# Rotary operands projected once in a four-layer diffusion transformer, with pair swaps on VectorE, sine products on GpSimd, and one exponential instruction a bank

## The reference, cut to what matters

```python
def _rope(x, sin, cos):
    xe = x[..., ::2]
    xo = x[..., 1::2]
    re = xe * c - xo * s
    ro = xe * s + xo * c
    return jnp.stack((re, ro), axis=-1).reshape(x.shape)
...
q = _rope(q, sq, cq)
k = _rope(k, sk, ck)
sim = jnp.einsum('bhnd,bhmd->bhnm', q, k) * DH ** (-0.5)
a = jax.nn.softmax(sim, axis=-1)
o = jnp.einsum('bhnm,bhmd->bhnd', a, v)
```

## Time and profile before

| what | value |
| --- | --- |
| median of 3 runs | 5925.9 us (5922.57 to 5927.59) |
| the profiled execution | 5942.8 us |
| its span, first to last instruction | 5941.0 us |
| mean granted TensorE clock | 0.951 of full speed |
| instructions | 164056 |
| busy share: TensorE, VectorE, ScalarE, GpSimd | 91%, 74%, 55%, 43% |
| HBM traffic | 19 GB/s over the span |

### The profile page before, as it was taken

One profiled execution on the slowest core, in us unless ns is written; L12 is line 12 of the kernel. 1 busy time (PEld: TensorE's weight loads), 2 busy tenths in 40 slices (PEclk: granted clock), 3 DMA queues, 4 the chain that ended last, 5 costly groups with the idle time before them and its releaser, 6 DMA issues. The chain is left out here.

```text
span 5941.0 us, 164056 instructions
## 1 busy us (share of the span) xinstructions
PE 5433.4 (91%) x66584; PEld 3128.8 (53%) x66584; DVE 4393.0 (74%) x6682; ACT 3259.3 (55%) x5626; POOL 2543.8 (43%) x2193
## 2 busy tenths in 40 slices
PE   5899999999999999999999999999989999999967
PEld 4554555555455455555545546565544545556442
DVE  6887776667888867576888886767788887767633
ACT  3455566565455566656455555655555555665634
POOL 2643535444344444444344344444534445344420
PEclk8998999999899999999999999999999999999975
DMA  4010010101001000010100101010100100101000
GB/s 104 12 40 17 14 29 9 37 12 41 18 16 43 13 26 19 21 25 17 43 13 26 31 11 34 12 32 15 35 22 14 38 17 15 29 10 36 10 17 6
DMA packets 282335, 145.67 MB, mean 25 GB/s; under 512 B 151517, under 2 KB 266813, under 8 KB 281470
## 3 DMA queue, kind: packets, MB, share of 16 engines
q1 hardware_dynamic: 281598, 135.17, 9.4%
HBM read 112.39 MB, written 3.01 MB: 19 GB/s over the span
## 5 line engine op out<-in xcount | busy, mean ns | idle before, releaser
L2459 DVE TENSOR_REDUCE max_part<-ring 128x2 f32<-128x800 f32 (+2 forms) x2304 | 2264.7, 1011 | 647.4 <-PE ring L1599 640.8
L2097 ACT ACTIVATE probs<-ring 128x1024 f32<-128x1024 f32 (+1 forms) x2048 | 1949.1, 969 | 1326.0 <-PE ring L1599 837.9
L1575 POOL TENSOR_TENSOR weight_sum<-weight_sum,probs 128x512 f32<-128x512 f32 (+1 forms) x1408 | 1825.2, 1296 | 350.4 <-ACT probs L2097 217.9
L1575 POOL TENSOR_TENSOR weight_sum<-probs 128x512 f32<-128x512 f32 x256 | 330.2, 1290 | 1984.6 <-ACT probs L2097 1564.5
L1599 PE MATMUL o_acc<-probs,region 128*64 128x256 f32 (+1 forms) x6656 | 908.3, 393 | 6.1 <-ACT probs L2097 3.2
L1599 PE MATMUL ring<-qop,region 64*128 64x256 f16 x9984 | 779.8, 271 | 22.8 <-DVE max_part L2459 8.2
L1599 PEld LDWEIGHTS ring<-qop,region 64*128 64x128 f16 x9984 | 450.8, 95 | 244.3 <-issue 118.8
L1599 PEld LDWEIGHTS o_acc<-probs,region 128*64 128x64 f32 (+1 forms) x6656 | 415.9, 137 | 281.3 <-issue 140.1
L1599 PE MATMUL o_acc<-probs,x_nv 128*32 128x256 f32 x6656 | 501.7, 420 | 37.0 <-ACT probs L2097 34.0
L1599 PE MATMUL ring<-shift_q,shift_k 64*128 64x256 f16 (+1 forms) x3840 | 529.8, 270 | 0.0
L2483 DVE RECIPROCAL o_inv<-ring 128x256 f32<-128x256 f32 x256 | 447.2, 1750 | 87.8 <-PE ring L1599 87.4
(11 more groups left out here) (191 smaller groups left out, 6966.3 us busy)
## 6 DMA issues: line engine op xcount, KB each, us to landing
stage<-in_wide SPq DMA_DIRECT2D x448, 64.0 KB, 2.0
nk<-x_nk SPq DMA_DIRECT2D x768, 25.0 KB
wo_stage<-in_wide SPq DMA_DIRECT2D x32, 512.0 KB, 4.0
ff_w<-in_ff_w SPq DMA_DIRECT2D x48, 256.0 KB, 3.5
stage<-in_wide SPq DMA_DIRECT2D x64, 128.0 KB, 2.6
v_stage<-in_wide SPq DMA_DIRECT2D x128, 64.0 KB, 2.0
ff_w<-in_ff_w SPq DMA_DIRECT2D x16, 512.0 KB, 3.7
v_stage<-kv_split SPq DMA_DIRECT2D x128, 48.0 KB, 1.7
```

The lines of the kernel that those rows point to most:

```text
L1575: pool.tensor_tensor(total, before, probs[0:rows_, (un.chunk + k) % PROBS, :], ALU.add)\
L2097: act.activation(to, src, ACT.Exp, scale=t.scale).then_inc(exp_done.sem, 2)
L2459: dve.tensor_reduce(dst, src, AX.X, ALU.max).then_inc(*release(one))
```

## The change

The change has five parts.

1. Each rotary operand is projected once. The swapped weights are no longer loaded or split; a rotary unit stages two pieces of weights instead of three, and `kv_in` for sub 1 is loaded in two parts instead of three.
2. VectorE makes the partners out of the one bank: `stream_shuffle` copies it to the new tile `swapped`, with neighbouring partitions exchanged, and the cosine product follows out of the same bank. Both tiles have two slots.
3. GpSimd multiplies `swapped` by the sines and then adds it to `raw`. ScalarE's high copy waits for that addition.
4. The exponential is one instruction a bank, 512 elements, and each bank is free when its own is done. Scores no longer need neighbouring banks; maxima still do.
5. The planner's costs follow these parts, and all tables of due times are replaced.

The diff, cut to its core:

```diff
-            return [("op", o, r) for r in range(2 if self.rope else 1)]
+            return [("op", o, 0)]
...
 AFTER = {
-    0: {"load": 1.499, "stats": 4.424, "ln": 4.629, "ctx": 0.522},
+    0: {"load": 2.2618, "stats": 4.2102, "ln": 2.1272, "ctx": 4.0025},
...
 PACE = {
-    0: 8.043, 1: 28.0, 6: 6.711, 7: 24.852, 3: 6.44, 4: 21.0, 9: 6.0, 10: 21.008
+    0: 9.5689, 1: 28.1233, 6: 7.0255, 7: 25.9515, 3: 7.0734, 4: 21.0636, 9: 6.0, 10: 21.0393
...
             if t.rope:
-                if k == 0:
-                    at = ROPE_OPS.index((n, i))
-                    before = ROPE_OPS[at - 2] if at >= 2 else None
-                    deps = [("DVE", ("job", before[0], low_job(UNITS[before[0]].t, before[1])))] if before else []
-                    self.part("DVE", "rope", due, one, 0.03 + w * 0.00142, [pe, *deps])
-                    return
-                self.part("DVE", "rope", (due[0], due[1] - 0.5), ("sin", n, j), 0.03 + w * 0.00142, [pe])
-                self.part("DVE", "rope", due, one, 0.05 + w * 0.00142, [("DVE", ("sin", n, j)), ("DVE", ("job", n, j - 1))])
-            self.part("ACT", "op", due, one, 0.17 + w * 0.00083, [("DVE", one) if t.rope else pe])
...
+                self.part("DVE", "rope", first, ("swap", n, j), 0.09 + w * 0.00112, [pe, *swapped])
+                self.part("DVE", "rope", due, ("cos", n, j), 0.03 + w * 0.00142, [pe, *free])
+                self.part("POOL", "rope", first, ("sin", n, j), 0.08 + w * 0.0025, [("DVE", ("swap", n, j))])
+                self.part("POOL", "rope", due, one, 0.08 + w * 0.0025, [("POOL", ("sin", n, j)), ("DVE", ("cos", n, j))])
+            self.part("ACT", "op", due, one, 0.17 + w * 0.00083, [("POOL", one) if t.rope else pe])
...
-            if paired(what):
+            if is_max(what):
                 r = min(side_by_side(), key=lambda r: beside(r) + beside(r + 1))
...
-                for k in range(sets):
-                    sp.dma_start(to[:, k, W_Q:W_Q + P].rearrange("p (h c) -> p h c", h=2),
-                                 src[:, k, SQ:SK].rearrange("p (h c) -> p h c", h=2)[:, :, 0:64])\
-                        .then_inc(stage_in[z].sem, 16)
+                sp.dma_start(to[:, W_Q:W_Q + P].rearrange("p (h c) -> p h c", h=2),
+                             src[:, SQ:SK].rearrange("p (h c) -> p h c", h=2)[:, :, 0:64])\
+                    .then_inc(stage_in[z].sem, 16)
...
-            sp.dma_start(kv_in[1][:, :, 1, :], a["wide1"][:, 0:DC, SKS:SO].rearrange("g p c -> p g c")).then_inc(kv_loaded[0], 16)
-            sp.dma_start(kv_in[1][:, :, 2, :], a["wide1"][:, 0:DC, SV:SQS].rearrange("g p c -> p g c")).then_inc(kv_loaded[0], 16)
+            sp.dma_start(kv_in[1][:, :, 1, :], a["wide1"][:, 0:DC, SV:SQS].rearrange("g p c -> p g c")).then_inc(kv_loaded[0], 16)
...
+                def turn(one):
+
+                    un, i = UNITS[one[1]], UNITS[one[1]].t.jobs[one[2]][1]
+                    z, w = raw_slot(un, i), N if i == 0 else un.t.kc[i - 1][1]
+                    if one[0] == "sin":
+                        a0 = 0 if i == 0 else un.t.kc[i - 1][0]
+                        pool.wait_ge(pair_swapped.sem, pair_swapped.at(un.n, un.t.rank(i) + 1))
+                        pool.tensor_tensor(swapped[:, z, 0:w], swapped[:, z, 0:w], rope_sin[:, a0:a0 + w], ALU.mult)\
+                            .then_inc(sin_ready.sem, 1)
+                        return
+                    pool.wait_ge(*taken(one))
+                    pool.wait_ge(sin_ready.sem, sin_ready.at(un.n, un.t.rank(i) + 1))
+                    pool.tensor_tensor(raw[:, z, 0:w], raw[:, z, 0:w], swapped[:, z, 0:w], ALU.add)\
+                        .then_inc(rope_step.sem, 1)
...
                 def exps(g):
-                    act.wait_ge(scores_full.sem, scores_full.at(n, c + 2))
+                    act.wait_ge(scores_full.sem, scores_full.at(n, c + 1))
...
-                    src = ring[0:r, b:b + 2, 0:nt * N].rearrange("p h (m q) -> p h m q", m=nt)
+                    src = ring[0:r, score_bank(g), 0:nt * N].rearrange("p (m q) -> p m q", m=nt)
...
-                    act.activation(to, src, ACT.Exp, scale=t.scale).then_inc(exp_done.sem, 2)
+                    act.activation(to, src, ACT.Exp, scale=t.scale).then_inc(exp_done.sem, 1)
...
                     if one[0] == "swap":
                         dve.wait_ge(*full(made))
                         if old:
 
                             dve.wait_ge(rope_step.sem, rope_step.at(old[0].n, old[0].t.rank(old[1]) + 1))
-                        dve.tensor_tensor(raw_sin[:, 0:w], v, rope_sin[:, a0:a0 + w], ALU.mult)\
-                            .then_inc(*release(made))
+                        dve.stream_shuffle(swapped[:, z, 0:w], v, PARTNER).then_inc(pair_swapped.sem, 1)
                         return
...
+                    dve.tensor_tensor(raw[:, z, 0:w], v, rope_cos[:, a0:a0 + w], ALU.mult).then_inc(*release(made))
```

203 lines of the change are left out of this document (99 added, 104 removed).

## The result

| | before | after |
|---|---|---|
| median of the runs, us | 5926.74 | 5846.36 (5841.76 to 5855.09) |
| ratio to before | | 0.9863 [0.9844, 0.9882] |
| span of the profiled execution, us | 5941.0 | 5846.5 |
| TensorE busy / not busy, us | 5433.4 / 507.6 | 5229.8 / 616.7 |

The kernel became 81 us faster where 272 were forecast; 5846 lies outside the range of 5550 to 5800. The first two lines are the page's busy line of the changed kernel and the shares by engine of the chain that ended last.

What follows compares the result with a forecast made beforehand. TensorE was taken to bound the kernel. Rotary stages 277, first stage 17 and start 3 saved, exponentials 25 lost: 272 us off the profiled 5942.8, less 16.9 to the median, gives 5654 us; eight in ten 5550 to 5800.

Steps and rivals of the forecast that it cites:

- TensorE thus sets the time in both: Rotary and other stages: TensorE, busy 353.3 of 382.6 us in a rotary stage, bounds both; VectorE at 82% stands close behind.
- The sum: Seven rotary stages: TensorE busy 318.0 plus 25 idle makes 343.0 instead of 382.6 us each, 277 us saved.
- The rival that named VectorE's maxima: Rotary stages: VectorE's maxima set them, or the new order loses the projection's gain; nothing comes of it, 5926 us; chance 0.04.
- GpSimd covered by TensorE: Rotary stages: GpSimd's two added passes, 833 us in all, stay below TensorE and are covered if pieces are made ahead.
- the rival that GpSimd eats half: Rotary stages: GpSimd and the port make pieces late and half the stages' gain goes, 139 us, giving 5793; chance 0.20.
- The port: VectorE's low halves (L2408) wait for GpSimd: 268 ns more each at 400 columns, 120 us in all, 15 a stage.
- The shuffle: VectorE's shuffle costs the same as the sine product, 562 ns at 400 columns, within 150 ns either way.
- The first stage: From 130 us to its end: 227 us instead of 235, GpSimd busy 223; with 9 in its sub-0 part, 17 saved.
- The exponentials: One a bank: ScalarE 330 us more, 25 us lost in all; bounds 50 less and 60 more.
- the prediction's sign that it is wrong: Stages of subs 6 and 7, without rotary embedding: a change of over 2% would show the forecast wrong.
- Due times: Planner's tables only reorder queues and can win or lose only idle time: 0, with 40 us either way.
- The clock: TensorE's granted clock in rotary stages at 0.96 or more; a fall from TensorE being fed more thinly would show it wrong.

Runs made afterwards that it cites:

- x6: Kernel before, order untouched, second projection of each rotary piece replaced by short stand-ins of two 64-column products side by side; 0.9944 of before.
- x7: Kernel before, order untouched, both projections kept, only VectorE's addition of the two products cut to 8 columns; 0.9862 of before.
- a_no_pool: Changed kernel without GpSimd's sine product and addition, order made anew; 0.9644 of before, 130 us below the changed kernel.
- x2: Kernel before, order untouched, second projection replaced by one short product of constants and VectorE's addition cut to 8 columns; 0.9778 of before.
- x3: Changed kernel, order untouched, GpSimd's sine product and addition cut to 8 columns each; 0.9695 of before, 100 us below the changed kernel.
- the square: Four kernels: old or changed rotary work, each with one exponential for two banks (1 and 1.0024 of before) or one per bank (0.9909 and 0.9863).
- n2_a_pace_big: Changed kernel with one number of its due-time tables moved by 0.1 us, no work changed; 0.9940 of before, 46 us above the changed kernel.
- b_split_fit: Kernel before with only the exponentials' part of the change, due-time tables searched for this form; 0.9909 of before, 54 us faster.
- x4: Kernel before, order and bank use untouched, each exponential of two banks cut into two instructions; 0.9995 of before.
- a_old_due: Changed kernel with all of before's due-time tables and the new costs; 1.0192 of before, 195 us above the changed kernel.

## Why the prediction was wrong

- **The step that failed first** is the end of the first part: "TensorE thus sets the time in both". It read the 92% as a bound and VectorE's 82% as standing behind. x6 and x7 show that in before a microsecond off TensorE was worth 0.25 and one off VectorE 0.5. So both were on the path; that VectorE's chain (wait for a piece, three passes, low part, then the maxima behind them in its queue) and TensorE's took turns is my reading of it. The sum converted 35.3 us a stage one to one. In its own terms, a stage of after is 29.7 us longer than forecast: TensorE's busy time is 333.0 instead of 318.0, and its idle time 39.7 instead of 25. Without GpSimd's passes (a_no_pool) both still miss, by 6.9 and 6.1 us. The change relieves VectorE too, and x2 suggests that TensorE's time then counts for more, so what this step alone cost is not fixed. The rival that named VectorE's maxima had 0.04; as "nothing comes of it" it was wrong too, since the change also relieves VectorE.
- **GpSimd covered by TensorE** (part 3) is the second. The size of the load was right: 255.8 us of a rotary stage, 265 forecast, 3327 in all against 3377. That it costs nothing was not: 100 us by x3, 130 by a_no_pool. This is the rival that GpSimd eats half, whose 139 us are near; but a_no_pool, at 211 us below before, still lacks 61 of the 272, though its first stage alone gained 44 us where 17 were forecast. The rest I put down to the first point, by argument.
- **The port** was sized wrongly. Low halves were forecast above 1.0 us at 400 columns and took 773 ns, less than before's 892, while GpSimd worked more. One by one, in the trace of before, the 93 of 192 that do not begin during a GpSimd operation take 573 ns on average and none over 581; the 99 that do take 1191. After the change GpSimd is busier and more begin during one, 130, as one would expect; but these take only 873. What went is the worst case, which needed VectorE's own addition ahead of the low half. It stands in the first three lines, of before: GpSimd's operation begins during VectorE's addition (L2438), and the low half (L2408) behind it ends only after that operation. The last two are the same place in x7, with an addition of 8 columns: the low half takes 0.57 us, and the GpSimd operation that begins during it 1.57.

```profile
555.78 0.57 DVE L2438 TENSOR_TENSOR raw<-raw,raw_sin 128x256 f32<-128x256 f32 x1
556.14 1.34 POOL L1575 TENSOR_TENSOR weight_sum<-weight_sum,probs 128x512 f32<-128x512 f32 x1
556.27 1.65 DVE L2408 TENSOR_TENSOR region<-raw,region 128x400 f16<-128x400 f32 x1
...
537.10 0.57 DVE L2408 TENSOR_TENSOR region<-raw,region 128x400 f16<-128x400 f32 x1
...
537.23 1.57 POOL L1575 TENSOR_TENSOR weight_sum<-weight_sum,probs 128x512 f32<-128x512 f32 x1
```

The 53 low halves directly behind an addition fall from 1147 to 628 ns in x7, which is most of its fall of the mean from 892 to 715. With GpSimd's passes on 8 columns (x3) 54 begin during a GpSimd operation, and the mean is 690. The Trainium skill, page "SBUF — State Buffer", section "Who interferes with whom", has a VectorE instruction with two SBUF inputs and a GpSimd instruction that reads SBUF exclude each other, and these traces agree. The forecast scaled the 322 ns with GpSimd's share; it depends on who comes second, and how often.
- **The shuffle** at 608 ns, 46 above the sine product, lay within its bounds. VectorE ended at 283.5 us a rotary stage (290 forecast).
- **The first stage**: 17 us saved were forecast, 13 were lost. From 130 us to its end it was to take 227 us with GpSimd busy 223 of them; it took 248 with GpSimd busy 219.78 (the window below, for the earlier trace rows). The load was right, but a share of 98% was not reached, and x3's 26 us are the price of the passes there.

```profile
130.00:378.00 248.00, 199.19 (x2259) 124.30 (x2257) 164.68 (x302) 100.53 (x218) 219.78 (x200) 0.84 0.04 12
```

- **The exponentials** had the wrong sign. 330 us more for ScalarE were forecast, 146 came (2095.4 against 1949.1), since short ones in a row overlap. 25 us lost were forecast; the square gives 54 gained without the rest and 95 with it, each side blurred by its tables. The bound of 50 gained was too near. That banks come free sooner is the likely cause and was not tried by itself. The 42 us that the other stages won (2662 to 2620) hang on the order and not on them alone (n2_a_pace_big, b_split_fit). So the prediction's sign that it is wrong, if those stages change by over 2%, was close to being met at 1.6%.
- **Due times** at 0 with 40 either way: 46 for one number, 109 and 195 for whole tables.
- **The clock** was expected at 0.96 or more in rotary stages as they filled; it was 0.93 to 0.96. With thinner work TensorE had more gaps, and in the two stretches shown above it ran at 1.2 GHz behind them; the prediction had named this as a sign of being wrong. Removed work was 261.6 us by the groups, but TensorE's busy time fell by 203.6: 58 us came back as slower records. By the prediction a rotary stage now has the same TensorE work as the others; it takes 333.0 us of busy time there and 308.3 in those.

The forecast's errors together: of 272 us, 130 went to GpSimd's passes (a_no_pool stands 211 below before). The exponentials, forecast at 25 lost, brought 54 to 95. If the parts simply add up, the projection and VectorE's addition, forecast at 297, brought some 211 - 95 = 116 to 211 - 54 = 157. x2, which takes both out in the old order (with stand-ins of 146 us), gained 132. That they add up is not shown, and the due times alone can move each of these by some 50 us.

## What to carry to other kernels

Before costing work off the busiest engine one to one, look at whether the second engine is above 80% in the same stage and feeds it: shorten each alone to a few columns, in an unchanged order, and read what a microsecond of each is worth. Work added to an engine at 69% of a stage is not free when it is in a chain that the others wait for, and a relieved TensorE can give part of its gain back as time at half clock. Where the order is written out, refit it for every variant, and count into the range what a small move of it does (here 46 us for one number).

## What the runs showed of the hardware that was not expected

- Two exponentials in a row overlap: 598 ns long each, 538 ns of ScalarE time each (128x512). Cutting one of 1023 ns in two added 62 ns of ScalarE's busy time in x4 (1910.7 us against 1800.1 for 1792 of them), and not 159.
- Whether a VectorE subtraction of two SBUF tiles (128x400) is long is decided where it begins: 573 ns on average and at most 581 outside a GpSimd operation, 1191 ns on average when it begins during one (before). It is longest where the GpSimd operation itself began during VectorE's own two-tile addition just ahead. Even an 8-column addition took 389 ns on average in x7.
- A shuffle of 128x400 float32 out of a bank took 608 ns, a product of the same size 555. On GpSimd the addition took 1167 ns at 400 columns where the product took 1015, but at 401 columns both took the same, 1036 and 1041.
- The same 64280 matmuls took from 5183.8 us (x3, mean clock 0.952) to 5357.4 us (a_old_due, 0.920) of TensorE time: their price goes with the clock that was granted.
